# The reciprocal root of the layer norm moved from ScalarE and VectorE to one GpSimd power

## The reference

```python
xn = (x - mean(x)) / sqrt(var(x) + 1e-5)              # over the 256 values of a token
qkv = xn @ W_qkv.T + b_qkv                            # 16 heads of 16
s = softmax(q @ k.T / 4 - slope * |distance|) @ v @ W_out.T + b_out
routed = sum over the 2 chosen experts of weight * (silu(xn @ w_gate) * (xn @ w_up)) @ w_down
shared = (silu(xn @ sw_gate) * (xn @ sw_up)) @ sw_down
out = x + s * silu(routed + shared)
```

## Time and profile before

| | us |
|---|---|
| median of 3 runs | 1720.38 (1719.31 to 1724.28) |
| span of the profiled execution, the only time of its own that is given | 1754.1 |
| TensorE busy in it | 1621.1 (92%) |
| ScalarE busy | 1437.5 (82%) |
| VectorE busy | 1027.0 (59%) |
| GpSimd busy | 495.5 (28%) |

### The profile page before, as it was taken

How to read it: one execution, slowest core, us unless ns; L and a number is a source line. 1 busy time by engine, 2 the same in 40 slices (tenths; PEclk the granted TensorE clock), 3 DMA queues, 4 the chain that set the end, 5 groups by cost and what they waited for, 6 DMA issues and landing times. The chain is left out here.

```text
span 1754.1 us, 40413 instructions
## 1 busy us (share of the span) xinstructions
PE 1621.1 (92%) x15531; PEld 694.1 (40%) x15533; DVE 1027.0 (59%) x2709; ACT 1437.5 (82%) x1822; POOL 495.5 (28%) x477
## 2 busy tenths in 40 slices
PE   5898997999999999999999999999999999999987
PEld 3555563233333333333333433333334333322355
DVE  7788767888734454445544444444444444577596
ACT  5778778988988988888888888888888888999911
POOL 1222230000033332333334333333343333222043
PEclk9999998999999999999999999999999999999998
DMA  6858774233364345444444544444445544467595
GB/s 204 266 183 264 261 217 129 62 107 86 85 181 134 99 132 151 123 127 119 131 119 118 143 131 118 125 125 126 112 121 146 146 124 125 130 188 224 179 318 174
DMA packets 197877, 265.34 MB, mean 151 GB/s; under 512 B 87968, under 2 KB 155088, under 8 KB 197424
## 3 DMA queue, kind: packets, MB, share of 16 engines
q1 hardware_dynamic: 165040, 171.44, 35.2%
q0 software_dynamic: 24192, 82.86, 15.5%
q10 hardware_dynamic: 8448, 8.39, 1.4%
HBM read 180.27 MB, written 90.46 MB: 154 GB/s over the span
## 5 line engine op out<-in xcount | busy, mean ns | idle before, releaser
L1421 ACT ACTIVATE probs_att<-SC_att 128x1024 f32<-128x1024 f32 (+10 forms) x1434 | 1195.4, 941 | 147.0 <-PE SC_att L1304 139.8
L1330 PE MATMUL O_att<-probs_att,V_att 128*32 128x512 f32 (+7 forms) x8168 | 711.7, 438 | 38.7 <-DVE probs_att L1448 15.3
L1448 DVE TENSOR_TENSOR probs_att<-probs_att,decay 128x128 f32<-128x128 f32 x1024 | 270.4, 286 | 362.6 <-ACT probs_att L1421 336.6
L1261 POOL DMA_INDIRECT ys<-ys_att,back_of_att x144 | 147.3, 1023 | 471.2 <-DVE ys_att L1512 345.5
L1330 PEld LDWEIGHTS O_att<-probs_att,V_att 128*32 128x32 f32 x8168 | 180.8, 110 | 212.7 <-issue 137.4
L1304 PE MATMUL SC_att<-Q,K_turned_att 64*128 64x512 f16 (+7 forms) x1328 | 243.1, 315 | 20.2 <-ACT probs_att L1421 8.6
L1304 PE MATMUL SC_att<-Q,K 64*128 64x512 f16 (+8 forms) x1243 | 223.2, 307 | 7.5 <-DVE K_turned_att L1435 5.2
L1304 PEld LDWEIGHTS SC_att<-Q,K_turned_att 64*128 64x128 f16 x1328 | 72.9, 93 | 301.3 <-ACT probs_att L1421 214.8
L1255 POOL DMA_INDIRECT x<-xn,row_of_att x144 | 140.3, 974 | 125.7 <-ACT probs_att L1421 93.8
L1249 POOL DMA_INDIRECT x<-w_rows,owner x72 | 72.0, 999 | 299.8 <-DVE row_of_att L1495 212.3
L660 POOL TENSOR_TENSOR inverse<-qk_tok,inverse 128x512 f16<-128x512 f32 x64 | 75.5, 1188 | 173.6 <-ACT inverse L692 166.5
(11 more groups left out here) (199 smaller groups left out, 1660.9 us busy)
## 6 DMA issues: line engine op xcount, KB each, us to landing
K<-k_stack SPq DMA_DIRECT2D x86, 256.0 KB
Q<-q_stack SPq DMA_DIRECT2D x86, 256.0 KB
x<-ys POOLq DMA_DIRECT2D x32, 512.0 KB, 5.0
x<-in_x SPq DMA_DIRECT2D x24, 512.0 KB, 6.6
k_stack<-inverse SPq DMA_DIRECT2D x96, 128.0 KB
q_stack<-inverse SPq DMA_DIRECT2D x96, 128.0 KB
inverse<-k_stack SPq DMA_DIRECT2D x42, 256.0 KB
inverse<-q_stack SPq DMA_DIRECT2D x42, 256.0 KB
```

Of the source, the lines that this page charges most:

```text
L1261: nc.gpsimd.indirect_dma_start(keep["ys"], index(back_of[:, t, i:i + 1]), ys[:, i % 2, t, :], None).then_inc(ys_out[i % 2], 16)
L1330: mm = pe.matmul(O[VW * g:VW * (g + 1), col:col + width * len(mine)], V[par][:, k, :], spans[:, j0:j0 + BPB * (len(mine) - 1) + 1:BPB, :], ...
L1421: nc.scalar.activation(probs[home][:, side + chunk.base:side + chunk.base + chunk.width], SC[:, c % SLOTS, start:start + chunk.width], ACT ...
L1448: v.tensor_tensor(diag, diag, decay[:, head_of(chunk.head), :], ALU.mult).then_inc(faded, 1)
```

## The change

GpSimd raises `var` to the power -0.5 in one TENSOR_TENSOR (L654 of the new program) against a constant tile `power_of` of -0.5, straight into `rstd`. ScalarE's 16 Sqrt and VectorE's 16 reciprocals are gone. ScalarE calls `warm_up` once, at the start, and keeps that table until the stage's end. GpSimd does `root(0)` ahead of the first maximum, `root(1)` behind it, and `root(j + 2)` at the start of block `j`.

```diff
@@ gpsimd
+                def root(j):
+                    pool.wait_ge(var_ready, j + 1)
+                    nc.gpsimd.tensor_tensor(rstd[:], var[:], power_of[:], ALU.pow).then_inc(rstd_ready, 1)
+
+                root(0)
                 pool.wait_ge(peaked, 1)
                 top_of(0, 0, 3)
+                root(1)
                 for j in range(NBLK):
+                    if j + 2 < NBLK:
+                        root(j + 2)
                     if j == SCALE_AT:
@@ scalar
-                def root(j):
-                    act.wait_ge(var_ready, j + 1)
-                    nc.scalar.activation(std[:], var[:], ACT.Sqrt).then_inc(std_ready, 1)
 ...
                 act.wait_ge(marks_set, 1)
-                root(0)
+                warm_up()
 ...
-                root(1)
                 for j in range(NBLK):
-                    if j + 2 < NBLK:
-                        root(j + 2)
-                        warm_up()
@@ vector
                 def ln_apply(j):
-                    dve.wait_ge(std_ready, j + 1)
+                    dve.wait_ge(rstd_ready, j + 1)
                     if j > 1:
                         dve.wait_ge(turned, j - 1)
                         dve.wait_ge(xn_stored[j % 2], 16 * (j // 2))
-                    ln(v.reciprocal(rstd[:], std[:]))
 ...
+                v.memset(power_of[:], -0.5)
```

More of the change, by code:

```diff
@@ L359, in tokens_stage @@
         var = r.sb("var", [P, TT])
-        std = r.sb("std", [P, TT])
+        power_of = r.sb("power_of", [P, TT])
         rstd = r.sb("rstd", [P, TT])
@@ L385, in tokens_stage @@
         var_ready = r.sem("var_ready")
-        std_ready = r.sem("std_ready")
+        rstd_ready = r.sem("rstd_ready")
         xn_ready = r.sem("xn_ready")
@@ L790, in _ @@
                 v = nc.vector
-                ln = Steps(dve, ln_step, 3)
+                ln = Steps(dve, ln_step, 2)
                 once = Steps(dve, r.sem("dve_once"), 7)
@@ L842, in ln_stats @@
                     v.tensor_scalar(var[:], mv[:, :, 1], 1e-5, None, ALU.add).then_inc(var_ready, 1)
+                    ln.end()
                 def ln_apply(j):
-                    dve.wait_ge(std_ready, j + 1)
+                    dve.wait_ge(rstd_ready, j + 1)
                     if j > 1:
@@ L852, in ln_apply @@
                     ins.then_inc(xn_ready, 1)
-                    ln.end()
                 def take_qk(j, k):
```

## The result

| | before | after |
|---|---|---|
| median, us | 1718.01 (1712.74 to 1724.28) | 1721.70 (1714.34 to 1728.88) |
| executions | 20 | 20 |

The ratio is 1.0026, with an interval of 1.0013 to 1.0038: 4.5 us slower, 2.2 to 6.5. That is a difference the twenty executions can tell from zero, and smaller than the 0.3% at which the forecast drew its line.

What follows compares the result with a forecast made beforehand. TensorE bounds the late token stage, SyncE's queue the early blocks. Late maximum 3.4, earlier split -0.95, block 5 +0.7 give +3.15 us: 1720.38 becomes 1723.5 us, range 1714.5 to 1729.5.

Steps and rivals of the forecast that it cites:

- its signs: Profile after: maximum at 15 to 17 us, no table load 3 to 270, first store about 31, late blocks 14.28 apart.
- The first switch: GpSimd's library switch at the start, ahead of block 0's power: 7.4 us, ending at 7.9.
- The power: GpSimd's power, shown nowhere in the earlier profile: taken as 0.9 us, with ends of 0.1 and 1.2.
- The rival of a slow power: Power is a software routine of several microseconds, exposed in three places: at 3 us, 1729.8 us in all; chance 0.05.
- The second switch: GpSimd's switch between block 0's power and the first maximum: ends at 15.6, making the maximum 3.4 us late.
- first rival: Slower: start switches lengthened by full DMA traffic, deciding from 1.25 times; 1725.8 us, or 1729.3 at 1.5 times; chance 0.18.
- The earlier split in block 0: Without a table load, ScalarE's split, the subtraction and the queue's start come 0.95 us earlier.
- Block 5: Power ahead of the exposed switch, less VectorE's reciprocal: +0.7 us on the SyncE queue's release at 116.45.
- ScalarE's 41.6 us: Table loads, Sqrt and Silu removed from 14 blocks: worth nothing except in block 0, 3.4 us as the bound.
- The second rival: Faster: ScalarE's 2.97 us a block was on the early blocks' path; half of 21.5 us back, 1712.8 us; chance 0.12.
- VectorE's cover: VectorE's 0.69 us wait for TensorE in a late block hides the slower apply: price zero, 2 us if gone.
- The powers of blocks 0 and 1 in VectorE's way: For block 1, the power replacing Sqrt and reciprocal on VectorE's path: +0.5 us at most, left in the range.

Runs made afterwards that it cites:

- after again: The changed kernel, unchanged, run again on another chip: 1758.08 us against 1755.79 for before, ratio 1.0011.
- E2: The changed kernel with a Sqrt of a constant tile, the Silu and their table loads put back on ScalarE in 14 blocks: 1.0016 of before.
- E3: The kernel before with one GpSimd power of constants, result unread, ahead of the first maximum: 1757.87 us against 1756.46, ratio 1.0011.
- E7: The changed kernel with the second maximum on TensorE and VectorE, so no library switch in block 5: 1750.97 us against 1755.79 for before, ratio 0.9953.
- E9: E1 with one GpSimd power of constants, result unread, ahead of the first maximum: 1720.44 us against 1713.84 for E1; 1.0014 of before.
- E1: The changed kernel with the roots of blocks 0 and 1 back on ScalarE and VectorE: 0.9985 and 0.9987 of before on two chips.
- E8: E1 with ScalarE's Sqrt, Silu and two table loads a block put back as ballast: 1715.99 us against 1713.84 for E1; 0.9999 of before.
- E5: E1 with the second maximum on TensorE and VectorE, so no library switch in block 5: 0.9915 and 0.9925 of before on two chips.

## Why the prediction was right

It forecast +3.15 us and no change that 0.3% could show; measured were +4.5 (2.2 to 6.5) and, on the other kind of chip, +1.9 (-1.6 to +5.6). The mechanism was the one named: a library switch stands bare ahead of the first maximum, and ScalarE's 42 us bring next to nothing. That the number came so near is in part luck, as the terms show. Of its signs, no table load came between 3 and 270 us, TensorE was busy for 61.0 us of 120 to 190 (61.4 before), and the first store came at 33.01 and 32.23, not at 31. The terms of the sum, one by one:

- **The first switch** was set to end at 7.9. It was over before the variances: the power started at 6.83, 0.08 us after VectorE's 6.58 + 0.17. The term was too large by at least 1 us. Block 5's 6.31 and 6.90 are not a price from the program's first instruction on.
- **The power** was set at 0.9 and took 1.04; 16 of them have a mean of 1.017. The rival of a slow power fell. Its bounds were 0.1 and 1.2, and the row of the same engine was the better guide than ScalarE's Sqrt.
- **The second switch** was set at 6.8 and took 8.71, and 8.07 to 8.20 in the five other traces that have it (after again, E2, E3, E7 and E9). That is 1.28 to 1.38 times the 6.31 of block 5. In 8 to 14 us the DMA engines are full (365 GB/s), as forecast. So one of the two switches is longer by more than the first rival's edge of 1.25. Whether the DMA traffic does it is not shown. For it: 8.07 to 8.71 at a DMA share of 1.09, 5.88 to 7.13 in block 5 for the same switch at 0.73. Against it: the switch back in block 5 took 7.56 us while the DMA engines had next to nothing to do (0.10, 37 GB/s, the row below), and the one at the start is also the first to the maximum's library in the program. No run took the two apart. The two misses cancelled in part: the maximum, forecast at 15.6, started at 16.58, and at 15.77 to 16.00 in the five others.

```profile
110.50:118.00 7.50, 7.50 (x76) 5.18 (x75) 5.40 (x16) 6.00 (x10) 0.01 (x1) 1.00 0.10 37
```

- **The earlier split in block 0** (-0.95) came as -0.15: the first store is 4.25 late with the maximum 4.40 late. VectorE waited 1.19 us for the power of block 1, where in before it waited 0.27 us for ScalarE's root. In E1, without that power, the split's gain is there: with the maximum 0.15 later the first store is 0.69 earlier. By the differences under E9 the split is worth 0.86 us, near the forecast, and the powers take 0.71 of it away. The prediction had seen this wait and left it in the range.
- **Block 5** was set at +0.7. From the store of block 4 to that of block 5 it is 119.30 - 95.92 = 23.38 us after and 116.45 - 94.74 = 21.71 before: +1.67. The power's 1.01 is in it; the switch back took 7.56 instead of 6.90. In E1's two traces the step is 22.23 and 21.07, in the two of before 21.71 and 20.98: +0.3 in the mean. Over all traces that keep block 5's switches it is 22.1 in the seven with powers and 21.0 in the three without. The term has the right sign and order, and the scatter allows no more.
- **ScalarE's 41.6 us** were priced at nothing. The medians and ratios of E2 and E8 put them at -2 to +2 us, with intervals of some 4 us to either side, and E8 shows the same stores up to block 4 with the loads and without. The second rival, half of the 21.5 us, fell. (The 74 us set beside the 42 leave out 14 x 0.4 us of Sqrt and Silu; with them they are 80.)
- **VectorE's cover**: the apply went from 642 to 685 ns a step, toward the 3.06 us a block that I expected at the upper end, and VectorE's wait for TensorE in a late block is 0.42 us instead of 0.69:

```profile
228.38 0.69 DVE L888 TENSOR_REDUCE stat<-GU_tok 96x4 f32<-96x512 f32 x1 [0.42 <-PE GU_tok L610]
```

The cover holds, and the late blocks are 14.28 apart. It is thin: in the second trace of after VectorE has no wait left at 214.81, and that block takes 217.42 - 203.02 = 14.40 us.

- **The powers of blocks 0 and 1 in VectorE's way** were left in the range (+0.5 at the most). They take 0.71 us at the first store, which is more; whether they take more than that later on is open.

By the ratios the budget closes in another way than it was written. The two roots at the start cost 1.0026 - 0.9987 = 0.0039 (6.7 us) on one kind of chip and 1.0011 - 0.9985 = 0.0026 (4.6 us) on the other. At block 15 it is 259.8 - 254.0 = 5.8 us, by the means of two traces each; 4.0 to 4.9 of it are there at the first store. The prediction had 3.4. The rest of the change gives back 0.0013 to 0.0015, 2.2 to 2.6 us, and 3.3 at block 15, where the prediction had -0.25. Of these four ratios only 1.0026 is clear of 1 with its interval, and on the slower chips the intervals of E1 and after overlap a little; on the faster they lie apart, as all the traces do. So both parts were probably forecast too small, with opposite signs, and the sum came out near by luck.

What the second part is made of stays open. E8, which has ScalarE's loads again, is at block 15 still 3.0 us ahead of before, but level with it in time (0.9999). What is left between E8 and before are VectorE's 14 reciprocals, 14 x 0.169 = 2.4 us by the earlier trace rows, that Sqrt no longer waits for VectorE in ScalarE's row, and where in a block the loads stand. In block 0 this is worth 0.84 us from the maximum to the first store (15.74 for 16.58). No run took these one at a time.

The Trainium skill ("GPSIMD Engine Reference", Key points) has GpSimd and VectorE share SBUF interfaces; the pair of 1.37 and 3.06 us above, the same four instructions with the subtraction behind them or beside them, agrees. By it alone after would be slower; with 14.28 us between the late blocks, as in before, TensorE hides it there.

## What to carry to other kernels

A library switch of GpSimd costs only where it stands between two instructions that are both ready: ask of each whether the engine would have waited there anyhow, and put the first use of a new library behind a wait that is longer than the switch, never ahead of the one instruction on which all weights hang. When work is moved to an engine that alternates between libraries, count the pairs of switches that it makes, and try to do a small maximum over partitions with a turn on TensorE and a reduction on VectorE instead; here that was worth 8 to 12 us (three long executions of E7 are not explained). A forecast that comes out near may be a sum of two misses: here the undone part (E1) told more than the whole.

## What the runs showed of the hardware that was not expected

- The switch to the maximum took 5.88 to 7.13 us in block 5 (DMA share 0.73 in before) and 8.07 to 8.71 us at the start (1.09, 365 GB/s); the switch back took 6.72 to 7.56 us in block 5, with the DMA engines nearly idle (0.18 in before, 0.10 in after). The first one of the program took at most 6.58 - 0.45 = 6.1 us in three traces, and nothing bounds it from below.
- A power of GpSimd on four columns takes 1.02 us, nearly as long as its subtraction of 512 columns (1.18 us). What it takes on more columns no run shows.
- Taking 42 us of table loads from ScalarE lengthened VectorE's apply, from 33.3 to 40.8 us (E8 to E1), by bringing GpSimd's subtractions beside it.
- Chips differ by 2.3% in pace: before takes 1715.7 and 1718.0 us on some and 1755.8 and 1756.5 on others. The token stage doesn't differ beyond the scatter (E5 has block 15 at 245.07 on the slower kind and 245.72 on the faster, E1 at 253.18 and 254.85). The mean granted clock of the traces is 0.984 to 0.988 on the slower kind and 0.989 to 0.992 on the faster, 0.3% apart; that is too little for 2.3%, and the rest is open.
